# Causal attention in the last two chunks: probabilities of two cells added on GpSimd, one ones product for both

## The chip, the cores and the metric

One Trainium2 chip, one NeuronCore of it. The metric is the device time of one execution in microseconds (us). TensorE, VectorE, ScalarE, GpSimd and SP (which only issues DMAs here) run their own instruction queues, each in order, and wait for one another on semaphores.

## The reference, cut to what matters

```python
x = L0_attn_src                                      # (1, 2048, 128)
x = x + 0.5 * _L0_ffn_ref(_layernorm(x), ...)        # blockwise fp4, 352 wide
x = x + _L0_attn_ref(_layernorm(x), ...)             # linear attention, 16 heads of 64, and its MLP
x = x + 0.5 * _L0_ffn_ref(_layernorm(x), ...)        # fp4 again
x = x + 0.5 * _L1_ffn_ref(_layernorm(x), ...)        # relu layer, 512 wide
xe = _layernorm(x)
x = x + _L1_attn_ref(xe, ...)                        # causal, 16 heads; q = xe (8 a head), v of 32 a head
#   scores = q @ k.T + mask; attn = softmax(scores); o = attn @ v; xe + gelu(o) @ Wf + bf
x = x + 0.5 * _L1_ffn_ref(_layernorm(x), ...)
```

## The kernel before, in words

Rows of x are 16 tiles of 128. What every engine does is one list, `PLAN`, worked out on the host: `follow` walks it on each engine, and each engine issues its part of every step in that order. `first_pass` is fp4 and the sums of linear attention, `second_pass` (by `SECOND_ORDER`) the rest of linear attention with fp4 and relu layer of earlier tiles beside it, `causal` everything from there on.

Causal attention works on 4 chunks of 512 queries and 4 groups of 4 heads in a chunk: groups 0 to 15. A cell `(g, kb)` is group g against one block of 128 keys; chunk c has 4(c+1) blocks, so `CELLS` has 160 cells, and `GROUP_U[g]` is the first cell of a group (0, 4, 8, 12, 16, 24, 32, 40, 48, 60, 72, 84, 96, 112, 128, 144, 160). The last four cells of a group lie on the diagonal and have 512, 384, 256 and 128 queries. Each cell is two halves of two heads: `scores` (L1653, bf16 into a pair of PSUM banks, mask at L1660) and the exponential on ScalarE (L967, 1024 columns into `pr`, a ring of 3 cells). `values` (L1677: four heads side by side, each 32 columns of the array, fp32) is issued in the first half of the next iteration for the cell before, `sums` (L1692: the same with ones, for the softmax's denominators) in its second half. `values` adds in bank 6, `sums` in bank 7, over a group.

The softmax's maximum is found ahead: `max` (L1618, mask L1624) makes the scores the other way round, up to 512 keys by two heads, and VectorE reduces them (L1290). The `max` steps of a group are spread over the cells of the group before, ending `MAX_LEAD` = 4 cells before its first cell. `row_max` (L1300 to L1304, VectorE) joins them and splits the maximum in two bf16 parts, `turn_max` (L1636) turns them, ScalarE copies (L975), and four DMAs (L654) put them beside the queries.

Scores, maxima and most single steps (`IN_SETS`) take three pairs of PSUM banks in turn, in plan order (`set_of`); a step waits until the reader of the step three before is done.

Behind a group, `take_o` (L982) and `take_d` (L988) copy the banks out; denominators are gathered by DMA (L663), inverted (L1308), stored and spread (L670, L677), and GpSimd multiplies (`norm`, L803). `gelu` (L996), `wf` (L1706), and the relu layer (`f_stats`, `d_norm`, `d_turn` L1555, `d_hidden` L1565 and L936, `d_out` L1576, `d_add`) follow for each chunk. Keys and values of a chunk come from `e_stats`, `e_norm` (L1089), `e_turn`, `e_k`, `e_v`, `split`; `store_parts` and `load_queries` on SP (L627, L635, L645) store the bf16 parts and load keys and queries. SP's queue takes these, `load_maxima`, `gather_sums`, `store_inverse`, `spread_inverse` and the stores of x in plan order. Whatever fp4 and relu work of tiles 8 to 15 the second pass left is put by `last_tiles` into half-cell slots from -17 on (`TAIL_START`, `TILE_STEPS`); negative slots stand before the first cell.

## Time and profile before

| what | value |
|---|---|
| runs of the kernel | 1080.92, 1081.2, 1095.3 us; median 1081.2 |
| profiled execution | 1089.29 us, its span 1087.5 us |
| granted TensorE clock, mean | 0.948 |
| PE busy (matmuls) | 920.0 us, 85% |
| VectorE, ScalarE, GpSimd busy | 713.5, 513.0, 257.8 us |
| first exponential of a cell | 463.8 us |
| `take_o` of groups 7, 11, 14, 15 | 668.4, 850.3, 1013.8, 1053.7 us |

The device time includes some 2 us around the span. Times of rows are counted from the span's start. L12 is line 12 of the kernel; PE is TensorE's matmul, PEld its weight load, DVE VectorE, ACT ScalarE, POOL GpSimd, SPq the DMA issues of SP. Many instructions have operands in one big tensor, `arena`. "<-" at the end of a row names what ended the idle time before it.

### The profile page before, as it was taken

What the parts mean: (1) busy time and instruction counts of PE and PEld (TensorE: products, weight loads), DVE (VectorE), ACT (ScalarE), POOL (GpSimd) and SP (SyncE); (2) the same over time, 40 slices, a digit from 0 to 9 for tenths busy, and PEclk for the clock granted to TensorE, in tenths of its full rate; (3) what the DMA queues carried; (4) which work ended last, traced back from release to release, by engine and by line L of the source; (5) the groups of instructions that cost most, each with busy time, mean ns of one, the idle gap of its engine ahead of it and who ended that gap; (6) DMA issues with size and microseconds to landing.
All of it is one profiled execution on the core that took longest, in us unless ns stands there. A gap on an engine that the chain in (4) does not pass through costs nothing.

```text
span 1087.5 us, 19966 instructions
## 1 busy us (share of the span) xinstructions
PE 920.0 (85%) x7332; PEld 459.6 (42%) x7353; DVE 713.5 (66%) x1675; ACT 513.0 (47%) x884; POOL 257.8 (24%) x405
## 2 busy tenths in 40 slices
PE   2788888778888687798889899899899989999986
PEld 1444446565676466444323333233322223332225
DVE  7899953468876666775755588566488757676012
ACT  1133332234444232354565556656556656566772
POOL 1546420045554555421311001112000000000000
PEclk9999998999998887988999899999899999999997
DMA  5300000000000040041002300001500000000000
GB/s 183 67 14 1 1 0 1 1 1 1 1 2 1 1 79 10 2 81 20 23 11 58 54 8 24 2 12 35 74 2 11 12 1 15 7 10 5 12 2 10
DMA packets 30935, 23.20 MB, mean 21 GB/s; under 512 B 9609, under 2 KB 27897, under 8 KB 30840
## 3 DMA queue, kind: packets, MB, share of 16 engines
q1 hardware_dynamic: 29928, 21.39, 9.1%
q8 instruction: 61, 1.00, 0.4%
q10 hardware_dynamic: 912, 0.54, 0.2%
q14 instruction: 34, 0.28, 0.1%
HBM read 17.32 MB, written 4.34 MB: 20 GB/s over the span
## 4 chain that ended last, share of the span: by engine, by line
PE 61%; DVE 16%; ACT 7%; POOL 6%; issue 5%; DMA 3%; SPq 1%; ACTq 0%; DVEq 0%; POOLq 0%
PE psum L1677 11%; PE psum L1692 10%; PE psum L1653 7%; DVE arena L1290 5%; PE psum L1618 5%; PE psum L1565 3%; PE psum L1412 3%; PE psum L1371 2%; ACT arena L967 2%; PE psum L1576 2%; PE psum L1534 2%; PE psum L1422 2%; POOL rs L697 2%; DMA arena<-arena 2%; PE psum L1599 2%
## 5 line engine op out<-in xcount | busy, mean ns | idle before, releaser
L1290 DVE TENSOR_REDUCE arena<-psum 128x2 f32<-128x1024 f32 (+2 forms) x320 | 336.3, 1063 | 146.6 <-PE psum L1618 83.2
L967 ACT ACTIVATE arena<-psum 128x1024 f32<-128x1024 f32 (+3 forms) x320 | 286.7, 898 | 169.3 <-PE psum L1653 95.6
L697 POOL TENSOR_TENSOR rs<-ve,mhalf 128x1 f32<-128x1 f32 x128 | 70.7, 559 | 389.3 <-DVE ve L1084 388.8
L1677 PE MATMUL psum<-arena 128*32 128x512 f32 (+3 forms) x1280 | 153.2, 551 | 1.3 <-ACT arena L967 1.3
L1692 PE MATMUL psum<-arena,ones 128*32 128x512 f32 (+3 forms) x1280 | 153.7, 553 | 0.0
L1618 PE MATMUL psum<-arena 48*128 48x512 bf16 (+3 forms) x640 | 114.2, 358 | 25.9 <-ACT arena L967 13.8
L1653 PE MATMUL psum<-arena 50*128 50x512 bf16 (+3 forms) x640 | 116.8, 361 | 11.6 <-DMA arena<-arena 4.0
L1653 PEld LDWEIGHTS psum<-arena 50*128 50x128 bf16 x640 | 31.1, 93 | 200.8 <-issue 135.1
L936 ACT ACTIVATE rh<-psum,fb 128x128 f32<-128x128 f32 x128 | 36.5, 370 | 60.9 <-PE psum L1565 56.9
L803 POOL TENSOR_TENSOR arena<-arena 128x512 f32<-128x512 f32 x15 | 19.1, 1274 | 188.2 <-DMA arena<-scr_sums 188.2
L1371 PE MATMUL psum<-WguT,xqT 128*128 128x352 f32 x128 | 52.1, 536 | 7.0 <-DVE hb L1115 5.8
L1618 PEld LDWEIGHTS psum<-arena 48*128 48x128 bf16 x640 | 36.0, 94 | 46.2 <-ACT arena L967 19.3
L1565 PE MATMUL psum<-xdT,fW 128*128 128x128 f32 x256 | 43.1, 322 | 7.7 <-DVE arena L1290 3.7
L701 POOL TENSOR_TENSOR xv<-xv,xm 128x128 f32<-128x128 f32 x32 | 20.2, 631 | 123.0 <-DVE xv L1042 123.0
L1565 PEld LDWEIGHTS psum<-xdT,fW 128*128 128x128 f32 x256 | 38.2, 228 | 20.2 <-issue 15.8
L1677 PEld LDWEIGHTS psum<-arena 128*32 128x32 f32 x1280 | 25.4, 109 | 43.1 <-issue 38.3
L1338 PE MATMUL psum<-bias_rows,onesb 128*128 128x128 bf16 (+1 forms) x107 | 28.7, 268 | 12.5 <-ACT arena L996 4.3
L855 ACT ACTIVATE th<-psum 128x352 f32<-128x352 f32 x32 | 14.9, 464 | 49.9 <-PE psum L1371 49.8
L1576 PE MATMUL psum<-fW,rh 128*128 128x128 f32 x256 | 38.0, 295 | 0.0
L1462 PE MATMUL psum<-arena 128*128 128x256 f32 x128 | 37.4, 390 | 0.0
L1692 PEld LDWEIGHTS psum<-arena,ones 128*32 128x32 f32 x1280 | 25.5, 109 | 24.8 <-issue 20.1
L1392 PE MATMUL psum<-WdT,hqT 128*128 128x128 f32 (+1 forms) x192 | 32.6, 314 | 2.7 <-ACT hqT L849 2.7
(186 smaller groups left out, 1494.9 us busy)
## 6 DMA issues: line engine op xcount, KB each, us to landing
arena<-scr_parts SPq DMA_DIRECT2D x96, 64.0 KB
arena<-scr_sums SPq DMA_DIRECT2D x60, 64.0 KB, 2.0
scr_parts<-arena SPq DMA_DIRECT2D x12, 256.0 KB, 2.6
arena<-arena SPq DMA_DIRECT2D x124, 2.0 KB, 1.7
X<-in_L_attn_src_dram SPq DMA_DIRECT2D x4, 256.0 KB, 4.9
out_dram<-X SPq DMA_DIRECT2D x16, 64.0 KB, 1.6
arena<-in_c_zsel_dram SPq DMA_DIRECT2D x1, 512.0 KB, 3.8
arena<-in_L_attn_Wk_dram SPq DMA_DIRECT2D x1, 512.0 KB
```

Of the source, the lines that this page charges most:

```text
L697: v.tensor_tensor(rs[:, u, t:t + 1], ve[:, u, t:t + 1], mhalf[:, :], ALU.pow).then_inc(s_rstd[u], 1)
L936: v.activation(rh[:, n % 2, j, :], bank(bank_d(n, "d_hidden"))[:, P * j:P * j + P], ACT.Relu, bias=fb1[:, j:j + 1]).then_inc(s_relu, 1)
L967: v.activation(pr[:, u % RING, pp, :, 0:CH - off], both(("scores", n))[0][:, :, off:CH], ACT.Exp).then_inc(s_p, 1)
L1290: v.tensor_reduce(MXP[:, j, 2 * pp:2 * pp + 2, m], both(("max", g, pp, j, m))[0][:, :, 0:hi - lo], AX_X, ALU.max).then_inc(s_mxd, 1)
L1371: last = mm(bank(b + k)[:, 0:GI], xqT[:, n % 2, :], WguT[:, k, :], start=True, stop=True)
L1462: last = mm(o, Wq[:, P * j:P * j + P], XNT[:, GRP * g:GRP * g + GRP], start=False, stop=True, skip_group_check=True)
L1565: last = mm(bank(b)[:, P * j:P * j + P], fW1[:, P * j:P * j + P], xdT[:, n % 2, :], start=True, stop=True)
L1576: last = mm(bank(b)[:, P:2 * P], rh[:, n % 2, j, :], fW2[:, j, :], start=False, stop=(j == FJ - 1), skip_group_check=True)
L1618: last = mm(o[:, par, 0:w], QS[c % 2][r, hp, P * j:P * j + P], KK[m][r, hp, 0:w], start=True, stop=(m < c), skip_group_check=True)
L1653: last = mm(o[:, par, off:CH], KK[kb // TPC][r, hp, P * (kb % TPC):P * (kb % TPC) + P], QS[c % 2][r, hp, off:CH], start=True, stop=(kb < T ...
L1677: last = mm(bank(O_BANK)[VD * h:VD * h + VD, off:CH], V[kb // TPC][:, kb % TPC, GH * (g % GPC) + h, :], pr[:, u % RING, h // 2, h % 2, 0:C ...
L1692: last = mm(bank(D_BANK)[VD * h:VD * h + VD, off:CH], ones1[:, 0:VD], pr[:, u % RING, h // 2, h % 2, 0:CH - off], start=(kb == 0), stop=en ...
```

## The change

In chunks 2 and 3 (but for the last four cells of group 15) GpSimd adds the probabilities of a cell to those of the cell before (`add_probs`, two operations a pair of cells, planned at the second cell plus one), and `sums` runs once for the pair, in the second half of the iteration four behind its first cell. `pr` becomes a ring of 5, `GT` a ring of 6 groups, and `DN` shares its place with tables that are used up. `d_norm` and `e_norm` of the last part, and the two small operations that split `row_max`, go from VectorE to GpSimd. `gelu` is by group. `store_parts` and `load_queries` of a chunk go behind the maxima of the third group of the chunk before. The last part starts at slot -12: the maxima of group 1 no longer end before the first cell, tiles 12 to 15 start at slots 2, 6, 12, 18 at two slots a step, and inversions and norms come two cells later. In the second pass `e_stats` and `e_norm` of the first tiles move a little.

```diff
-                ("e_stats", 8, 1), ("den", 0), ("x_stats", 0, 1), ("x_turn", 1, 1), ("d_add", 6, 1),
-                ("e_norm", 8, 1), ("quotients1", 0, 1),
...
+                ("den", 0), ("x_stats", 0, 1), ("x_turn", 1, 1), ("d_add", 6, 1), ("e_stats", 6, 0),
...
-NORM_AT, GELU_AT = 4, 7
-RELU_START, RELU_TILE = 12, 4
+PAIRED_FROM = 2
+SUM_AT = 4
+INVERT_AT, NORM_AT, GELU_AT = 4, 6, 9
+RELU_START, RELU_TILE = 14, 4
+HELD = 6
...
-TAIL_START = {8: -16, 9: -16, 10: -15, 11: -14, 12: -17, 13: -11, 14: -7, 15: -2}
-MAX_START = {0: -16, 1: -8}
-SECOND_KEYS_START, SECOND_KEYS_EVERY = -12, 3
+FIRST_SLOT = -12
+TAIL = {8: (-11, 1), 9: (-11, 1), 10: (-10, 1), 11: (-9, 1), 12: (2, 2), 13: (6, 2), 14: (12, 2), 15: (18, 2)}
+MAX_LEADS = {1: 2, 2: 3, 3: 3, 4: 3}
+SECOND_KEYS_START, SECOND_KEYS_EVERY = -9, 3
...
-        RING = 3
+        RING = 5
...
+        SUMS = sorted([(a + (SUM_AT if pair else 1), a, pair)
+                       for g in range(MGROUPS) for a in range(GROUP_U[g], GROUP_U[g + 1])
+                       for pair in [g // GPC >= PAIRED_FROM and (g + 1 < MGROUPS or a < GROUP_U[g + 1] - TPC)]
+                       if not pair or (a - GROUP_U[g]) % 2 == 0])
...
+            max_end = [FIRST_SLOT + len(MAXES[0])] + [2 * GROUP_U[g] - 2 * MAX_LEADS.get(g, MAX_LEAD)
+                                                     for g in range(1, MGROUPS)]
+            for g in range(MGROUPS):
+                lo = max_end[g - 1] if g else FIRST_SLOT
                 for k, x in enumerate(MAXES[g]):
-                    slots.setdefault(MAX_START[g] + k, []).insert(0, ("max", *x))
...
+                    slots.setdefault(lo + (max_end[g] - lo) * k // len(MAXES[g]), []).append(("max", *x))
+                slots.setdefault(max_end[g], []).append(("row_max", g))
+                slots.setdefault(max_end[g], []).append(("turn_max", g))
+                if g % GPC == GPC - 2 and g + 2 < MGROUPS:
+                    slots[max_end[g]] += [("store_parts", g // GPC + 1), ("load_queries", g // GPC + 1)]
...
+            for a in PAIRED:
+                for pp in range(GP):
+                    put(a + 2, "add_probs", GP * PAIRED.index(a) + pp)
...
+                out += [x for x in here if x[0] in ("gelu", "add_probs")]
                 cut = (len(others) + 1) // 2
                 for i in range(GP):
+                    slot = slots.get(2 * u + i, [])
+                    out += [x for x in slot if x[0] == "row_max"]
                     if u < len(CELLS):
                         out.append(("scores", GP * u + i))
...
+                    out += [x for x in slot if x[0] == "max"]
+                    if i == 0 and 0 < u <= len(CELLS):
+                        out.append(("values", u - 1))
...
+                    for when, a, _ in SUMS:
+                        if (i, u) == (1, when):
+                            out.append(("sums", a))
...
+                    out += others[cut * i:cut * (i + 1)] + [x for x in slot if x[0] not in ("row_max", "max")]
...
+            def add_probs(n):
+
+                a, pp = PAIRED[n // GP], n % GP
+                w = [CH - P * max(kb - TPC * (g // GPC), 0) for g, kb in CELLS[a:a + 2]]
+                into = pr[:, a % RING, pp, :, w[0] - w[1]:w[0]]
+                pool.wait_ge(s_av, a + 1)
+                pool.wait_ge(s_p, GP * (a + 1) + pp + 1)
+                v.tensor_tensor(into, into, pr[:, (a + 1) % RING, pp, :, 0:w[1]], ALU.add).then_inc(s_ps, 1)
...
+            def row_max_parts(g):
+                pool.wait_ge(s_mxr, g + 1)
+                k = me.did(v.tensor_copy(MXH, MXS[:, :, :, 0]))
+                me.wait(k)
+                v.tensor_tensor(MXS[:, :, :, 1], MXS[:, :, :, 0], MXH, ALU.subtract).then_inc(s_mxn, 1)
...
-                if u >= RING:
-                    act.wait_ge(s_dn, u - RING + 1)
+                old = u - RING
+                if old in SUM_N:
+                    act.wait_ge(s_dn, SUM_N[old] + 1)
+                elif old >= 0:
+                    act.wait_ge(s_ps, GP * (PAIRED.index(old - 1) + 1))
+                    act.wait_ge(s_av, old + 1)
...
+                if u in PAIRED:
+                    pe.wait_ge(s_ps, GP * (PAIRED.index(u) + 1))
+                else:
+                    pe.wait_ge(s_p, GP * (u + 1))
```

## Rows read from the trace of the kernel before

**Rows 1.** Stretches: length; busy us of PE, PEld, DVE, ACT, POOL; clock; DMA share; GB/s
```profile
700.00:800.00 100.00, 93.36 (x844) 36.04 (x842) 59.93 (x82) 55.72 (x86) 13.72 (x23) 0.97 0.18 33
1000.00:1050.00 50.00, 48.74 (x450) 11.77 (x450) 3.33 (x7) 37.23 (x42) 1.28 (x1) 1.00 0.03 7
```

**Rows 2.** The same view, the stretch around the first cells
```profile
420.00:540.00 120.00, 98.48 (x971) 53.28 (x969) 85.81 (x195) 50.68 (x110) 37.56 (x58) 0.88 0.15 28
```

**Rows 3.** Groups of lines, 849-1012 us: busy, mean ns | idle before, releasers
```profile
L1290 DVE TENSOR_REDUCE arena<-psum 128x2 f32<-128x1024 f32 (+3 forms) x89 | 100.1, 1126 | 41.2 <-PE psum L1618 27.5 <-PE psum L1624 13.3
L967 ACT ACTIVATE arena<-psum 128x1024 f32<-128x1024 f32 (+3 forms) x95 | 90.0, 952 | 49.6 <-PE psum L1653 38.7 <-PE psum L1660 10.8
```

**Rows 4.** Instructions in time, one half-cell of group 12: start, duration, engine, line
```profile
885.65 0.39 PE L1653 MATMUL psum<-arena 50*128 50x512 bf16 x2
887.19 0.39 PE L1653 MATMUL psum<-arena 50*128 50x512 bf16 x2
887.42 0.38 PE L1618 MATMUL psum<-arena 48*128 48x512 bf16 x2
887.62 1.02 ACT L967 ACTIVATE arena<-psum 128x1024 f32<-128x1024 f32 x1 [0.52 <-PE psum L1653]
887.73 1.06 PE L1677 MATMUL psum<-arena 128*32 128x512 f32 x8
```

**Rows 5.** The same view, group 14: an exponential, and scores that waited for it
```profile
1010.22 0.60 ACT L967 ACTIVATE arena<-psum 128x512 f32<-128x512 f32 x1 [0.46 <-PE psum L1660]
1010.89 0.10 PEld L1653 LDWEIGHTS psum<-arena 50*128 50x128 bf16 x2 [0.62 <-ACT arena L967]
```

**Rows 6.** Chain that ended last, group 15: start, duration, what
```profile
1019.18 0.32 PE psum L1653 x2
1019.51 0.99 PE psum L1692 x8
1049.90 0.78 PE psum L1677 x8
1053.32 0.38 PE psum L1677 x8
```

**Rows 7.** Groups of lines of GpSimd, each shape apart
```profile
L701 POOL TENSOR_TENSOR xv<-xv,xm 128x128 f32<-128x128 f32 x32 | 20.2, 631 | 123.0 <-DVE xv L1042 123.0
L803 POOL TENSOR_TENSOR arena<-arena 128x512 f32<-128x512 f32 x15 | 19.1, 1274 | 188.2 <-DMA arena<-scr_sums 188.2
L783 POOL TENSOR_TENSOR X<-X,xe 128x128 f32<-128x128 f32 x16 | 7.2, 453 | 27.5 <-DVE xe L1089 27.4
L743 POOL TENSOR_TENSOR arena<-arena 127x1024 f32<-127x1024 f32 x1 | 2.4, 2355 | 0.0
L714 POOL CAST ident<-arena 128x64 bf16<-128x64 f32 x1 | 0.2, 237 | 0.0
```

**Rows 8.** Waits of TensorE's weight loads, 667 to 1053 us: total, times, longest
```profile
PEld psum L1636 <- DVE arena L1304: 3.4, 4, 0.8
```

**Rows 9.** Chain that ended last, 590 to 612 us, and a wait of that stretch
```profile
588.46 2.75 DMA scr_parts<-arena
591.22 0.29 SPq L635
595.40 0.64 SPq L654
597.35 7.90 DMA arena<-arena
...
PEld psum L1653 <- DMA arena<-arena: 4.5, 1, 4.5
```

**Rows 10.** VectorE in time around 771 us, and TensorE's wait
```profile
776.87 0.25 DVE L1308 RECIPROCAL arena<-arena 128x16 f32<-128x16 f32 x1 [5.23 <-DMA arena<-arena]
...
PE psum L1565 <- DVE arena L1290: 3.7, 1, 3.7
```

**Rows 11.** Chain that ended last, behind the last cell
```profile
1056.19 1.28 ACT L996
1057.48 0.64 ACT arena L996
```

142 lines of the change are left out of this document (74 added, 68 removed).

## Prediction

> **What bounds the kernel now.** I read the stretches first, then the groups of lines of the late part, then single instructions in order of time, then the waits. In the last two chunks TensorE is busy 93 to 97% of the time at nearly full granted clock, ScalarE 56 to 74%, VectorE 60% and in the last group 7% [rows 1]. The mean exponential and the mean row-maximum reduction each take about a microsecond, and both engines' idle time there is ended by TensorE [rows 3]. So from 667 us to 1053 us TensorE's queue is the bound. In the instructions, one half-cell runs scores, a maximum product, and `values` or `sums`, and the next half begins 1.54 us later [rows 4]. Scores plus maximum take 0.54 us of it (887.19 to 887.73), the four-head product 0.99 us, the pitch in the last group [rows 6]. Where no maxima are left a half-cell is 1.32 us [rows 6]. Ahead of that, from 420 to 540 us, nothing is full: TensorE 98.5 of 120 us at a clock of 0.88, VectorE 85.8 [rows 2]; that stretch is bound by handoffs.
>
> **Time base.** The profiled execution took 1089.3 us with a span of 1087.5; the median of the runs is 1081.2. All terms are differences in us, summed against 1089.3 and carried over to the median, 8.1 lower. A measurement of this kernel tells about 2%, 21.6 us, from no change.
>
> **1. One ones product for two cells.** Chunk 2 has 12 cells a group in four groups, chunk 3 has 16; all are paired but the last four cells of group 15: 24 + 24 + 6 = 54 pairs, so 54 of 160 sums go. A full one is worth 0.99; the last four cells of a group lose one of 384 and one of 128 columns, 0.78 + 0.38 [rows 6]. Groups 8 to 11: 4 x 0.99 + 1.16 = 5.1 each, 20.5. Groups 12 to 14: 6 x 0.99 + 1.16 = 7.1 each, 21.3. Group 15: 5.9. In all 47.7 of TensorE's queue.
>
> What is late once it is gone? The halves of a pair of cells are now scores-max-values, scores-max-sums, scores-max-values, scores-max. The fourth is 0.54 long. PSUM pairs rotate by three, so a maximum product takes the pair that the scores of the half before had. Those scores' exponential starts 0.43 behind them and takes 1.02 [rows 4], and the bank reaches TensorE 0.07 later (1010.82 to 1010.89) [rows 5]: 1.52 after the scores. In a full half the maximum comes at 1.54 + 0.23 = 1.77 and nothing waits; behind the short half it would come at 0.54 + 0.23 = 0.77, so it waits 0.75. TensorE takes its queue in order, so the whole queue waits. A pair gains 0.99 - 0.75 = 0.24. Full pairs with one maximum per half: 4 each in groups 8, 9, 10 and 6 each in 12, 13, 14, that is 30, so 7.2. The shorter cells on the diagonal have shorter exponentials; I take half of their 1.16 in six groups, 3.5. Group 11 has 32 maxima (the next group is of chunk 3) in 24 halves: 32 x 1.13 = 36 on VectorE [rows 3], as much as 24 halves of 1.54: nothing. In some short halves other steps (keys, relu layer) stand and fill the wait: 1. In group 15 `values` waits for the exponential of the half before, at 1.52 instead of 0.64: gain 0.11 in each of six pairs, 0.7. Term: **-12**. Bounds: 0, and -47.7 if no wait appears.
>
> **2. The additions on GpSimd.** Two of 128x1024 per pair. The nearest row is a two-input operation of 127x1024, 2.36; the 128x512 one is 1.27 [rows 7]. So 4.7 per pair, against 5.9 per pair of cells (6.16 - 0.24): GpSimd fits, with some 1.2 left. The sums come four cells behind the first cell of the pair, and a ring of five holds the tiles: the second addition ends 6.3 after the start of the pair's second cell, and three cells are 8.9. No wait there: **0**. The bound above is rival 4.
>
> What hangs on it is `row_max`. Its copy and subtraction go to GpSimd, and the plan puts the additions of cells U-6 and U-5 right ahead of them, U being the group's first cell. Counted from the start of cell U-5: `values` of cell U-6 ends at 1.6, so addition 0 runs 1.6 to 4.0 and addition 1 to 6.3, then two small operations (a cast of 64 columns is 0.24 [rows 7]) and handoffs, to 6.9. TensorE reaches `turn_max` after scores (2.08), maximum (1.54 + 1.52 = 3.06) and `values` (3.37 to 4.36), and stands until 6.9: 2.5 us, with scores, exponentials and all else of its queue behind it. Before, this wait cost 3.4 in four places in the whole late part [rows 8]. Other steps in that half (a layer's turn, a `wf`) cover some 0.4. Groups 9 to 15: 7 x 2.1 = **+15**. Bounds: 0 if GpSimd runs ahead of this, +25 if casts and handoffs take a microsecond more.
>
> Here the skill speaks against the change. The trace: on GpSimd a 128x128 two-input operation takes 0.63 beside VectorE's quantising chain and 0.45 in the other place [rows 7], 1.39 times. The Trainium skill (GPSIMD Engine Reference, Key points) says that GpSimd shares its SBUF interfaces with VectorE and is held up by VectorE instructions in a two-port mode or with two SBUF inputs. In the late part VectorE nearly only reduces out of PSUM [rows 3], which is neither, so I leave the additions at 2.36; with the factor it is rival 4.
>
> **3. Stores and loads of the keys, moved in SP's queue.** Before, they follow the last `split` of a chunk. Near 600 us the maxima of the next group are issued behind 12 loads and land after 7.90 us; TensorE waits 4.5 for them [rows 9], about 4.0 of it with nothing in flight (it ends at 605.25). Near 771 the gather of group 9's sums lands late, VectorE waits 5.23 for it, and TensorE 3.7 for VectorE [rows 10]. After, they are queued right behind a group's maxima, and the next gather is at least four cells off, over 15 us, against 2.8 for the stores and 24 issues of 0.3, 10 us, on the queue [rows 9]. Both waits go: **-8** (bounds 0 and -10). The spread of group 4's inverse now stands behind these loads, so `norm` waits on GpSimd; the turn that needs GpSimd next is four cells later, so 0 (at most +4).
>
> **4. First cells, tail and maxima rearranged.** Scores begin four slots after the first group's maximum row, and tiles 12 to 15 are spread over the cells behind at two slots a step. Work is the same; what can be gained is TensorE's 21.5 idle us of 420 to 540, and the half clock (0.12 x 120 = 14) [rows 2]. Against it: the rows of groups 0 to 4 have leads of two to four cells for a chain over VectorE, GpSimd, TensorE, ScalarE and four DMAs, of which the four issues of 0.64 alone take 2.5 [rows 9]. I take half the idle time: **-10**. Bounds: +8 (one such wait for each of four groups at 2) and -30.
>
> **5. Norms on GpSimd, gelu by group, invert and norm two cells later, e_norm order in the second pass.** The norms relieve VectorE of some 34 short operations, where it isn't the bound: 0 (-3 to +3, the relief or a turn that waits for GpSimd). Gelu has the same columns and the same table loads. At the end the table load (1.28) comes earlier but three gelus of 0.64 with it, so the first `wf` starts as before [rows 11]: 0.
>
> **Sum.** -12 + 15 - 8 - 10 = -15: 1089.3 to 1074, and 1081.2 to **1066**.
>
> **Rivals.**
> 1. The short half is free: part 1 pays in full, 36 more: 1030. For it: TensorE's all-idle time in this stretch is small now, and other steps may sit in the short halves more often. Against: the 1.52 of rows 4 and 5 can't shrink. Chance 0.12.
> 2. `turn_max` doesn't stand: GpSimd reaches the row early, or TensorE has as much other work. 15 less: 1051. For it: the leads leave room to be late. Against: the queue order. Chance 0.22.
> 3. The first part gives nothing (its tiles only fill cells that TensorE already fills), and the new stops lower the granted clock a little: +10 to +15, 1076 to 1083. For it: from 667 on a step moved in is a step added. Chance 0.20.
> 4. The slower side: the additions run beside VectorE at 1.39 x 2.36 = 3.28. From 2.95 on, two exceed 5.9 and GpSimd is the bound: 54 x (6.56 - 5.9) = 35, and `turn_max` 7 x 1.85 = 13 later; -15 + 48: 1114. Against: the fifteen 128x512 ones agree in mean with the 1024 one by size. Chance 0.08.
>
> The forecast (1058 to 1075) has 0.38. Left out of 1040 to 1088 are rivals 1 and 4, 0.20. Faster by over 2% (below 1059.6): rivals 1 and 2 and 0.04 of the forecast, 0.38. Slower: rival 4 and 0.02 of rival 3, 0.10. Within: 0.52.
>
> **What would show it.** Right: `sums` at about 106 cells' worth; a regular wait of some 0.75 of maximum products for the exponential, and cells of about 2.95 us; a wait of 2 us at the turn of groups 9 to 15 ended by GpSimd; additions of 2.36; no stop near 600 and 771; first exponential over 10 us sooner. Wrong: cells at 2.6 us (rival 1), no such wait at the turn (2), group 4 reached no sooner than before (3), additions over 2.95 (4).

## The result: slower by 5.2%, and the profile after

The changed kernel took 1142.6 us (median of 4 runs, 1134.6 to 1152.6), the kernel before 1081.1 beside it: a ratio of 1.052 (95% interval 1.040 to 1.063). The profiled execution took 1137.3 with a span of 1135.4. Forecast were 1066 and a range of 1040 to 1088; the sign was wrong too. Among runs of one kernel some are slower than the others by over 1.5%: the ratios leave these out, the medians don't.

Where the 47.9 us of span (1087.5 to 1135.4) went, by the starts of the first exponential of a group of cells (L967 before, L1022 after) and of the last `take_o`:

| stretch | before | after | difference | forecast |
|---|---|---|---|---|
| start to group 4 | 535.3 | 525.1 | -10.2 | -10 |
| groups 4 to 7 | 132.2 | 167.3 | +35.1 | -4 |
| groups 8 to 15 (the late part) | 386.2 | 407.6 | +21.4 | -1 |
| behind the last `take_o` | 33.7 | 35.4 | +1.7 | 0 |

The groups of lines, from the page of the kernel after (line, engine, operation, shapes, count, busy us, mean ns of one, idle time before and what ended it):

```profile
L832 POOL TENSOR_TENSOR arena<-arena 128x1024 f32<-128x1024 f32 (+2 forms) x108 | 222.1, 2074 | 114.1 <-PE psum L1735 88.1
L1752 PE MATMUL psum<-arena,ones 128*32 128x512 f32 (+3 forms) x848 | 105.0, 570 | 0.0
L1613 PE MATMUL psum<-ident,xd 128*128 128x128 f32 x32 | 10.8, 339 | 33.9 <-POOL xd L836 32.8
```

GpSimd now makes 108 additions; `sums` (L1752) has 848 products, 106 cells' worth. And TensorE stood 33 us ahead of a layer's turn, L1613, for a norm on GpSimd.

The late part as one stretch (us, busy time of each engine, then granted clock, DMA share, GB/s), of before and then of after, to be read against [rows 1]:

```profile
667.50:1053.70 386.20, 363.94 (x3374) 116.46 (x3374) 230.97 (x286) 242.18 (x311) 28.79 (x41) 0.98 0.07 15
```

```profile
692.40:1100.00 407.60, 331.92 (x2942) 111.08 (x2942) 224.79 (x260) 237.78 (x311) 262.15 (x175) 0.95 0.06 14
```

TensorE lost 432 instructions (54 pairs of eight) and 32.0 us of busy time. Its idle time (the stretch less busy) rose from 22.3 to 75.7, by 53.4. The difference is the +21.4. TensorE's waits there (engine, line, what it waited for: us in all, times, longest):

```profile
PE psum L1676 <- ACT arena L1022: 31.0, 41, 4.6
PE psum L1694 <- POOL arena L847: 20.6, 7, 5.8
PE psum L1735 <- ACT arena L1022: 7.5, 11, 0.9
```

The second is `turn_max` behind GpSimd. The first is the maximum product behind a short half, but not in all of the 41: two of them, 4.62 and 3.97 us, are TensorE waiting while ScalarE loads its table for the gelu of the chunk before, does it and loads the table back, and the kernel before has these two as well (3.98 and 3.97, in a row of 12.4 us in 16 times). The other 39 are 0.57 in the mean, and 0.72 where the short half ahead holds nothing but scores and a maximum product. The third is `values` waiting for its exponential; before the change that was 1.3 us. The row of before, one of the two gelu stops after, and two products behind short halves of group 12:

```profile
PE psum L1618 <- ACT arena L967: 12.4, 16, 4.0
...
730.54 1.28 ACT L1048 ACT_TABLE_LOAD   x1
731.83 2.19 ACT L1048 ACTIVATE arena<-arena 128x512 f32<-128x512 f32 x4
734.04 1.28 ACT L1022 ACT_TABLE_LOAD   x1
736.29 0.39 PE L1676 MATMUL psum<-arena 48*128 48x512 bf16 x2 [4.62 <-ACT arena L1022]
...
905.71 0.39 PE L1676 MATMUL psum<-arena 48*128 48x512 bf16 x2 [0.72 <-ACT arena L1022]
911.70 0.39 PE L1676 MATMUL psum<-arena 48*128 48x512 bf16 x2 [0.72 <-ACT arena L1022]
```

What one turn behind GpSimd looks like, in order of time (start, duration, what, [idle time before and its end]):

```profile
718.56 4.63 POOL L832 TENSOR_TENSOR arena<-arena 128x1024 f32<-128x1024 f32 x2
723.14 0.20 POOL L845 CAST arena<-arena 128x16 bf16<-128x16 f32 x1
723.42 0.22 POOL L847 TENSOR_TENSOR arena<-arena 128x16 f32<-128x16 f32 x1
...
723.70 1.02 PE L1694 MATMUL psum<-ident,arena 128*8 128x128 f32 x4 [5.80 <-POOL arena L847]
```

Two operations of 0.2 us stand behind 4.6 us of additions, and TensorE behind them. Stretches of six us before and after this stop show what it does to the clock (the last but two column):

```profile
711.90:717.90 6.00, 5.36 (x47) 1.56 (x39) 4.92 (x5) 3.95 (x5) 5.92 (x5) 1.00 0.01 3
723.70:729.70 6.00, 5.67 (x22) 1.54 (x23) 1.23 (x1) 1.60 (x2) 2.01 (x4) 0.50 0.01 1
```

Granted 1.00 before and 0.50 (1.2 GHz) after 5.8 us of standing still: 22 products in place of 47 in the same time.

Two stops ahead of the late part are larger than anything in the forecast. First the one near 472 us (TensorE and SP's queue in order of time):

```profile
465.24 1.47 SPq L650 DMA_DIRECT2D scr_parts<-arena  x3
468.96 4.12 SPq L658 DMA_DIRECT2D arena<-scr_parts  x12
473.12 4.14 SPq L668 DMA_DIRECT2D arena<-scr_parts  x12
...
487.78 0.72 PE L1676 MATMUL psum<-arena 48*128 48x512 bf16 x4 [15.47 <-DMA arena<-scr_parts]
```

Chunk 1's key loads are issued from 469 to 477 us, and the maxima of group 4 want them at 472.3. Second, the one from 603.4 to 626.6, of the same view:

```profile
599.35 4.12 SPq L658 DMA_DIRECT2D arena<-scr_parts  x12
603.51 4.97 SPq L668 DMA_DIRECT2D arena<-scr_parts  x12
608.53 0.66 SPq L693 DMA_DIRECT2D scr_sums<-arena  x1
621.09 1.71 SPq L700 DMA_DIRECT2D early<-scr_sums  x4
624.47 1.26 POOL L854 TENSOR_TENSOR arena<-arena,early 128x512 f32<-128x512 f32 x1 [24.74 <-DMA early<-scr_sums]
625.71 0.80 POOL L836 TENSOR_SCALAR xd<-X,mv,rs 128x128 f32<-128x128 f32 x1
...
626.57 0.47 PE L1613 MATMUL psum<-ident,xd 128*128 128x128 f32 x1 [23.20 <-POOL xd L836]
```

Read it upwards from the last row: TensorE's turn waits for a 0.80 us norm of the residual layer on GpSimd; that stands behind `norm` of group 4 (L854); that waits for the spread inverse; the spread was issued at 621.1, when the store of the inverse had landed; the store was issued at 608.5 behind 24 loads of keys. The DMA view of 596 to 624 us gives its landing (KB each, us from issue to landing), and above it the mean busy share of the DMA engines in 40 slices, in tenths:

```profile
DMA  9910004555555555555655555555555553000343
...
arena<-scr_parts SPq DMA_DIRECT2D x24, 64.0 KB
early<-scr_sums SPq DMA_DIRECT2D x4, 64.0 KB, 1.9
scr_sums<-arena SPq DMA_DIRECT2D x1, 8.0 KB, 12.5
```

The same 8 KB store lands in 1.4 us (median of the eight after it) with no loads before it.

### The profile page after: what moved, and what is told of

It is laid out like the page before. It is cut to its first block, busy times and chain, and to the rows that moved or that the text cites. A ratio compares the mean times of both kernels' runs of the same rounds, so it can differ in the third digit from the quotient of the medians.

```text
span 1135.4 us, 19349 instructions
## 1 busy us (share of the span) xinstructions
PE 880.4 (78%) x6900; PEld 449.0 (40%) x6921; DVE 694.8 (61%) x1609; ACT 507.7 (45%) x887; POOL 511.6 (45%) x579
## 4 chain that ended last, share of the span: by engine, by line
PE 50%; DVE 15%; POOL 12%; ACT 10%; issue 7%; DMA 3%; SPq 2%; ACTq 0%; POOLq 0%; DVEq 0%
PE psum L1735 9%; PE psum L1752 6%; DVE arena L1352 5%; PE psum L1711 5%; ACT arena L1022 4%; PE psum L1676 4%; POOL arena L832 4%; PE psum L1623 3%; PE psum L1470 3%; POOL rs L720 2%; PE psum L1429 2%; PE psum L1592 2%; PE psum L1480 2%; PE psum L1634 2%; PE psum L1657 2%
## 5 line engine op out<-in xcount | busy, mean ns | idle before, releaser
L1352 DVE TENSOR_REDUCE arena<-psum 128x2 f32<-128x1024 f32 (+2 forms) x320 | 335.3, 1063 | 219.0 <-PE psum L1676 118.1
L1022 ACT ACTIVATE arena<-psum 128x1024 f32<-128x1024 f32 (+3 forms) x320 | 282.1, 898 | 162.8 <-PE psum L1711 89.2
L832 POOL TENSOR_TENSOR arena<-arena 128x1024 f32<-128x1024 f32 (+2 forms) x108 | 222.1, 2074 | 114.1 <-PE psum L1735 88.1
L1752 PE MATMUL psum<-arena,ones 128*32 128x512 f32 (+3 forms) x848 | 105.0, 570 | 0.0
L1711 PEld LDWEIGHTS psum<-arena 50*128 50x128 bf16 x640 | 31.7, 93 | 176.9 <-issue 109.8
L1735 PEld LDWEIGHTS psum<-arena 128*32 128x32 f32 x1280 | 25.6, 109 | 46.9 <-issue 31.8
L724 POOL TENSOR_TENSOR hv<-hv,hm 128x352 f32<-128x352 f32 x32 | 29.8, 930 | 28.9 <-DVE hv L1098 28.9
L1613 PE MATMUL psum<-ident,xd 128*128 128x128 f32 x32 | 10.8, 339 | 33.9 <-POOL xd L836 32.8
```

The lines of the kernel that those rows point to most:

```text
L724: k = me.did(v.tensor_tensor(x, x, m, ALU.subtract))
L832: v.tensor_tensor(into, into, pr[:, (a + 1) % RING, pp, :, 0:w[1]], ALU.add).then_inc(s_ps, 1)
L1022: v.activation(pr[:, u % RING, pp, :, 0:CH - off], both(("scores", n))[0][:, :, off:CH], ACT.Exp).then_inc(s_p, 1)
L1352: v.tensor_reduce(MXP[:, j, 2 * pp:2 * pp + 2, m], both(("max", g, pp, j, m))[0][:, :, 0:hi - lo], AX_X, ALU.max).then_inc(s_mxd, 1)
L1711: last = mm(o[:, par, off:CH], KK[kb // TPC][r, hp, P * (kb % TPC):P * (kb % TPC) + P], QS[c % 2][r, hp, off:CH], start=True, stop=(kb < T ...
L1735: last = mm(bank(O_BANK)[VD * h:VD * h + VD, off:CH], V[kb // TPC][:, kb % TPC, GH * (g % GPC) + h, :], pr[:, u % RING, h // 2, h % 2, 0:C ...
```

## The experiments

Stages of the profiled executions, us. "Late" is from group 8's first exponential to the last `take_o`; idle is late less TensorE's busy time; stops are TensorE's longest near 470 and near 610; ratios are to the kernel before on the same chip, with the 95% interval. A dash is a stop that isn't there. The ratio of the changed kernel itself is known to 0.011, some 12 us. "By the ratios" below is the difference of two ratios, times 1083 us; where it is smaller than that, what an edit did is read from the stretches of the trace and not from the time.

| kernel | to group 8 | late | idle | end | stops | median | ratio |
|---|---|---|---|---|---|---|---|
| before | 667.5 | 386.2 | 22.3 | 33.7 | -, 4.0 | 1081.1 | 1 |
| after | 692.4 | 407.6 | 75.7 | 35.4 | 15.5, 23.2 | 1142.6 | 1.052 (1.040-1.063) |
| e1 | 678.9 | 409.5 | 72.8 | 33.0 | 14.6, 3.1 | 1123.3 | 1.040 (1.032-1.048) |
| e2 | 676.9 | 417.5 | 75.9 | 35.6 | 11.1, 6.5 | 1132.6 | 1.049 (1.043-1.055) |
| e4 | 692.0 | 396.6 | 65.0 | 35.7 | 13.8, 22.3 | 1127.4 | 1.043 (1.038-1.049) |
| e5 | 698.3 | 387.8 | 21.6 | 36.3 | 19.4, 24.8 | 1110.9 | 1.031 (1.023-1.038) |
| e6 | 677.3 | 412.6 | 75.7 | 35.6 | 6.2, 7.5 | 1122.8 | 1.033 (1.027-1.040) |
| e7 | 668.4 | 401.9 | 70.5 | 30.0 | 11.2, - | 1108.5 | 1.021 (1.017-1.026) |
| e8 | 680.5 | 382.2 | 19.2 | 31.7 | 14.5, 7.1 | 1090.7 | 1.005 (1.001-1.009) |
| e9 | 668.8 | 394.8 | 59.5 | 30.0 | 4.8, 4.5 | 1094.9 | 1.009 (1.006-1.012) |
| e10 | 676.1 | 377.9 | 55.5 | 33.4 | 12.9, 6.3 | 1089.2 | 1.003 (0.998-1.008) |
| e11 | 677.3 | 384.3 | 22.0 | 30.5 | -, 13.2 | 1097.1 | 1.014 (1.009-1.020) |
| e12 | 680.2 | 410.7 | 38.9 | 31.7 | 11.3, 5.6 | 1121.2 | 1.037 (1.032-1.043) |
| e13 | 677.2 | 413.0 | 75.7 | 35.6 | 14.2, 4.4 | 1126.8 | 1.043 (1.038-1.049) |
| e14 | 666.0 | 394.6 | 29.3 | 33.6 | -, 11.8 | 1095.7 | 1.010 (1.006-1.015) |
| e15 | 680.4 | 410.4 | 74.6 | 35.7 | 14.9, 4.9 | 1130.7 | 1.042 (1.036-1.049) |
| e16 | 691.3 | 379.5 | 55.6 | 36.6 | 15.0, 23.5 | 1117.8 | 1.029 (1.023-1.035) |
| e17 | 682.1 | 379.5 | 55.5 | 31.5 | 13.0, 7.3 | 1097.2 | 1.006 (1.001-1.011) |
| e18 | 670.0 | 378.6 | 56.5 | 31.8 | 3.9, 4.4 | 1083.7 | 0.997 (0.994-1.001) |
| e19 | 674.4 | 375.4 | 48.7 | 34.2 | 4.8, 6.3 | 1077.2 | 0.989 (0.985-0.992) |

One caution for the column "to group 8": e7, e8, e9, e10, e12 and e17 place keys, loads and norms of the first groups alike or nearly so, and their stop near 470 is 11.2, 14.5, 4.8, 12.9, 11.3 and 13.0. A single profile's front part can't be compared to better than some 10 us.

The table also shows what the turn waits cost beside their own length. In the six kernels that keep the row's split behind the additions on GpSimd (after, e1, e2, e6, e13, e15) the late part has 72.8 to 75.9 us idle and TensorE is busy 332 to 342 us of it, at a granted clock of 0.91 to 0.95. In the four that pair without these waits (e10, e16, e17, e18) it is 55.5 to 56.5 idle and 322 to 324 busy, at 0.98 to 0.99.

### First round: one part undone at a time

**e1, norms back on VectorE.**
```diff
-        POOL_NORMS = {x for x in PLAN[main:] if x[0] in ("d_norm", "e_norm")}
+        POOL_NORMS = set()
```


> The norms d_norm and e_norm of the last part go back to VectorE; all else as changed. Theory A (two stops in the first half of causal attention: 15.5 us at 472 us for key loads, 23.2 us at 603 us because d_norm stands on GpSimd behind norm, which waits for a DMA; they are the loss): the 23 us stop goes, the 15 us one stays, so about 22 us less than the changed kernel, some 1118 us. Theory B (the loss is the pairing itself in the last two chunks: additions, turn waits, short halves): within 5 us of the changed kernel.

19 us of the median came back, 13 by the ratios, less than the 22 expected. The 23.2 us stop shrank to 3.1, now for VectorE (the waits of 440 to 668 us):

```profile
PE psum L1676 <- DMA arena<-scr_parts: 14.6, 1, 14.6
PE psum L1613 <- DVE xd L1145: 3.1, 1, 3.1
```

The other stop, 14.6 us for the loads of chunk 1, has nothing to do with the norms.

**e2, stores and loads back behind the last `split` of a chunk.**
```diff
                         out.append((name, i - lag))
+                        if name == "split" and (i - lag) % TPC == TPC - 1:
+                            c = (i - lag) // TPC
+                            out += [("store_parts", c), ("load_queries", c)]
...
-                if g % GPC == GPC - 2 and g + 2 < MGROUPS:
-                    slots[max_end[g]] += [("store_parts", g // GPC + 1), ("load_queries", g // GPC + 1)]
...
```


> store_parts and load_queries go back behind the last split of their chunk, and the pace of the keys of chunks 2 and 3 is that of before; all else as changed. Theory A: chunk 1's loads are issued 3 cells sooner, the 15.5 us stop shrinks to under 3; group 4's inverse is stored and spread ahead of chunk 2's loads, so the 23.2 us stop goes too (in its place the old 4 us stop near group 6, for maxima behind loads): 30 to 35 us less, some 1106 us. Theory B: within 5 us.

A miss: 10 us by the medians, 3 by the ratios, in place of 30 to 35. Group 8 was reached 15.5 us sooner, and the late part was 9.9 longer. The 15.5 us stop turned into one of 11.1 a little earlier, where scores wait for the spread maxima (`arena<-arena` on SP) that were issued behind the same 24 loads; the 23.2 us stop into 6.5; and the one near 771 of [rows 10] came back larger, 9.0 near 797. In this place of the plan too, a small transfer that TensorE wants soon is behind the loads.

**e4, the split of the row maxima back on VectorE.**
```diff
                 v.tensor_reduce(MXS[:, :, :, 0], ..., AX_X, ALU.max, negate=True).then_inc(s_mxr, 1)
+                dve.wait_ge(s_mxr, g + 1)
+                me.wait(me.did(v.tensor_copy(MXH, MXS[:, :, :, 0])))
+                v.tensor_tensor(MXS[:, :, :, 1], MXS[:, :, :, 0], MXH, ALU.subtract).then_inc(s_mxn, 1)
...
```


> The two small operations that split the maximum row go back to VectorE; all else as changed. The wait at turn_max in groups 9 to 15 (20.6 us in 7 times) should fall to under 4 us: by both theories 15 to 18 us less than the changed kernel, some 1124 us. If the wait only moves (TensorE waits for something else later), the time is that of the changed kernel.

15 us less by the medians, 9 by the ratios. The late part fell by 11.0, and 8.4 us of turn waits stayed although GpSimd had nothing to do with the row any more. That left a question, answered by e7 and e10.

**e5, no pairs.**
```diff
-PAIRED_FROM = 2
+PAIRED_FROM = 4
```


> No cells are paired: one sums product per cell, no additions on GpSimd; all else as changed. Theory A with the forecast's terms for the late part (short halves leave -12 of 48, turn waits +15 and more): the pairing is worth nothing or costs up to 8 us, so 0 to 8 us less than the changed kernel, and the two early stops stay. Theory B: the loss is the pairing, 50 us less, some 1090 us. If the pairing pays as planned: up to 30 us more than the changed kernel.

Without what the change is about the kernel is 32 us faster by the medians and 23 by the ratios, and its late part is 387.8, as before the change. It missed what either theory gave, 0 to 8 and 50. So the pairing, in the form it has, costs some 20 us of the late part; the rest of the loss (1110.9 against 1080.5 beside it) lies in the front part.

### Second round: all side effects moved back

**e6, loads of keys placed elsewhere.** Chunk 1's behind group 1's maxima, chunk 2's behind the spread of group 4's inverse.
```diff
-                if g % GPC == GPC - 2 and g + 2 < MGROUPS:
-                    slots[max_end[g]] += [("store_parts", g // GPC + 1), ("load_queries", g // GPC + 1)]
+                if g in (1, 10):
+                    slots[max_end[g]] += [("store_parts", 1 + g // 5), ("load_queries", 1 + g // 5)]
+            slots.setdefault(2 * (GROUP_U[5] + INVERT_AT + 1) + 1, []).extend([("store_parts", 2), ("load_queries", 2)])
```


> Only two places change against the changed kernel: chunk 1's store and loads stand behind the maxima of group 1 (iteration 2 instead of 5), chunk 2's behind the spread of group 4's inverse (iteration 29 instead of 28). Queue theory: the 15 us stop falls to 5 or less, the 23 us stop falls to under 4 since the inverse is no longer behind the loads; 25 to 35 us less, 1108 to 1115 us. Rival (the DMA rings are simply loaded with the loads, whatever the order on SP's queue, and GpSimd's norm is late all the same): under 12 us less.

Both stops shrank (15.5 to 6.2, 23.2 to 7.5) and 20 us came back by the medians and the ratios, from the order of SP's queue alone. That is under the 25 to 35 expected: group 8 is reached 15.1 us sooner, and the late part is 5.0 longer. It is 2 to 10 us longer in every kernel of the table that has the early stops mended and the turn waits left (e1, e2, e6, e13, e15), with the same idle time and a lower clock. Why the clock is lower there no run shows.

**e7, e6 with the norms (e1) and the row's split (e4) on VectorE; the pairs stay.** **e8, the same without pairs** (`PAIRED_FROM = 4`).

> As the last one, and in addition the norms and the split of the maximum row go back to VectorE; pairs and additions stay. If the terms add up (stops 35, turn waits 11 to 15): 1095 to 1103 us. If one stop only gives way to the next: over 1110 us.

> As the last one without pairs: what is left of the change is the rearranged first part and small moves. Forecast term of part 4, -10 against the kernel before, and -4 for the stops that the kernel before had near 600 and 771: 1068 to 1076 us. Against e7 it shows what the pairing is worth when GpSimd does nothing else: my theory of late part (short halves hold TensorE 0.75 us, half the clock's gain lost) says e7 is 5 to 15 us slower than this; if pairing pays once the turn waits are gone, e7 is the faster.

e8 is within 1% of the kernel before: the rearranged first cells and tail by themselves gain nothing, where 9 to 17 us were expected. e7 is a miss as well, between its 1095 to 1103 and its 1110. It is 18 us slower than e8 by the medians, 17 by the ratios, and 19.7 in the late part of the profiles. So the pairing still lost time, though GpSimd had only additions to do. Its turn waits, 11.3 us in six times, were now put down to VectorE:

```profile
691.79 1.23 DVE L1353 TENSOR_REDUCE arena<-psum 128x2 f32<-128x1024 f32 x1 [0.64 <-PE psum L1686]
692.71 4.66 POOL L833 TENSOR_TENSOR arena<-arena 128x1024 f32<-128x1024 f32 x2
693.06 0.20 DVE L1363 TENSOR_REDUCE arena<-arena 128x16 f32<-128x48 f32 x1
693.29 1.81 DVE L1365 CAST arena<-arena 128x16 bf16<-128x16 f32 x1
695.14 2.26 DVE L1366 TENSOR_TENSOR arena<-arena 128x16 f32<-128x16 f32 x1
...
697.46 0.80 PE L1698 MATMUL psum<-ident,arena 128*8 128x128 f32 x3 [3.51 <-DVE arena L1366]
```

A cast and a subtraction of 16 columns take 1.81 and 2.26 us, and the subtraction ends with GpSimd's second addition (692.71 + 4.66 = 697.37, 695.14 + 2.26 = 697.40). The reductions in the same stretch, out of PSUM and of 48 columns of SBUF, take what they take without additions beside them (1.22 and 0.20).

**e9, e7 with the single steps of odd iterations in the second, short half.**
```diff
-                cut = (len(others) + 1) // 2
+                cut = 0 if u % 2 and u > GROUP_U[GPC * PAIRED_FROM] else (len(others) + 1) // 2
...
```


> As e7 (pairs stay), and in the odd iterations of the last two chunks every single step of the plan stands in the second half, which has no product of four heads. Theory: a short half waits 0.75 us for the exponential unless something else fills it, so some 20 of the 48 filled halves give 0.5 to 0.75 us each: 8 to 15 us less than e7. If the wait comes from something else (GpSimd, VectorE), the time is e7's within 3 us.

1094.9 (1092.6 to 1101.1), ratio 1.009 (1.006 to 1.012): 13.5 under e7, as expected. Of this the late part shows 7.1 (401.9 to 394.8): idle time fell by 11.0, and busy time rose by 3.9 (331.4 to 335.3) with the granted clock down from 0.96 to 0.94. So a step put where TensorE waits was nearly free.

### Third round: what the additions do to the rest

**e10, e7 with the additions cut to 8 of up to 512 columns a head.** It leaves out most of the sums of the second cells, so the denominators aren't the reference's; instructions, waits and handoffs are as in e7.
```diff
-                v.tensor_tensor(into, into, pr[:, (a + 1) % RING, pp, :, 0:w[1]], ALU.add).then_inc(s_ps, 1)
+                v.tensor_tensor(into[:, :, 0:8], into[:, :, 0:8], pr[:, (a + 1) % RING, pp, :, 0:8], ALU.add).then_inc(s_ps, 1)
```


> e7 with the additions cut to 8 columns of each head, so that they take some 0.3 us instead of 2.36; every wait stays. It leaves out most of the additions, so the denominators are too small. Theory C (the late part loses by TensorE's short half and by the granted clock that falls with it, GpSimd has nothing to do with it once the maximum row is split on VectorE): within 4 us of e7, 1104 to 1112 us. Rival D (the additions' length is what holds the ring of tiles, the sums or VectorE's memory port): most of the 18 us between e7 and e8 come back, 1091 to 1096 us.

19 us under e7 by the medians, 20 by the ratios: theory C fell, and rival D's amount came back. Turn waits 11.3 to 0.1, the late part 401.9 to 377.9, 24.0 less: 15.0 of idle time and 9.0 of busy time (331.4 to 322.4, the granted clock 0.96 to 0.98). The two small operations on VectorE, in e7 and then here:

```profile
L1366 DVE TENSOR_TENSOR arena<-arena 128x16 f32<-128x16 f32 x7 | 9.6, 1370 | 0.2
L1365 DVE CAST arena<-arena 128x16 bf16<-128x16 f32 x7 | 7.0, 995 | 0.2
```

```profile
L1365 DVE CAST arena<-arena 128x16 bf16<-128x16 f32 x7 | 1.3, 187 | 0.2
L1366 DVE TENSOR_TENSOR arena<-arena 128x16 f32<-128x16 f32 x7 | 1.2, 176 | 0.2
```

Eight and five times the duration, from the additions' width alone; e8, with no additions, has the same 187 and 176. Against e8 this is also the clean price of pairing without GpSimd's weight: busy 363.0 to 322.4 (-40.6), idle 19.2 to 55.5 (+36.3), net **-4.3**. The forecast's part 1 had -47.7, +36 and -12.

**e12, e7 with 47 products of 512 columns (four heads each, over a constant tile) put into the short halves.** They add to the denominators, which aren't the reference's.
```diff
+                        if (i, u) == (1, when + 1) and pair and LAST_SUM[CELLS[a][0]] != a:
+                            out.append(("filler", a))
...
```


> e7 with a ones product of 512 columns over a constant tile in every short half (47 of them, into the denominators' bank, so the denominators are wrong): TensorE gets back the 47 us of queue that the pairing had taken out, at the places where it now waits. Theory C: the filler takes the place of the 0.75 us wait and holds the clock up, so the time doesn't grow: e8's time within 5 us, 1086 to 1096 us, that is less than e7 although more is computed. Rival E (the clock plays no part, waits alone are the loss): the filler costs 0.99 for a wait of 0.75 to 0.9, so e7 plus some 5 us, 1110 to 1116 us.

1121.2 (1117.5 to 1124.4), 12.7 over e7 by the medians and 18 by the ratios, over what either theory gave (1096 and 1116). Had each cost its full 0.99, it would be 47. In the late part idle time fell from 70.5 to 38.9, busy time rose from 331.4 to 371.8, and the clock stayed at 0.96. So a short half has room for some 0.7 of an 0.99 product (31.6 of idle time in 47), and filling it didn't bring the clock back. The turn stops were still there (9.4 us), and where they are gone the clock is 0.98 (e10, e16).

**e13, the changed kernel with `norm` of group 4 five cells later.**
```diff
-                    put(end + NORM_AT, "norm", g)
+                    put(end + NORM_AT + (5 if g == 4 else 0), "norm", g)
```


> The changed kernel with one step moved: the norm of group 4 stands five cells later in the plan. Theory A: the 23 us stop is GpSimd waiting in this one norm for the spread inverse, which is behind chunk 2's loads; it goes, and the 15 us stop stays: about 20 us less than the changed kernel, 1114 to 1122 us. Rival: the loads themselves hold the kernel at that place (the next maxima, the next inverse), and the stop only moves: under 8 us.

1126.8 (1124.2 to 1130.5), ratio 1.043 (1.038 to 1.049): 16 us off the median, 9 by the ratios, with one instruction moved on GpSimd and nothing in the DMA queue; 20 were expected. The 23.2 us stop is gone, and two of 4.4 and 2.3 are left; group 8 starts at 677.2 in place of 692.4. The stop needs both: the late inverse that `norm` waits for, and the layer's `d_norm` queued behind `norm`.

**e11, the kernel before with chunk 2's loads at iteration 30, chunk 3's behind group 10's maxima, and the last gelu split by group.**
```diff
+                if g == 10:
+                    put(hi, "store_parts", 3)
+                    put(hi, "load_queries", 3)
+            put(30, "store_parts", 2)
+            put(30, "load_queries", 2)
...
```


> The kernel before with two small parts of the change alone: store and loads of chunk 2 at iteration 30 and of chunk 3 behind the maxima of group 10 (with the keys of chunk 3 paced to end there), and the last chunk's gelu of the three finished groups ahead of the last inversion. The stops at 601 us (4.0) and 774 us (3.7) should go, and the end behind the last cell should be some 3 us shorter as in e7: 7 to 11 us less than the kernel before. If the loads only collide with something else: no difference.

1097.1, ratio 1.014 (1.009 to 1.020), 1.4% slower where 7 to 11 us less were expected: a 13.2 us stop at 612.7, where VectorE's reciprocal waits for a gather behind the 24 loads.

```profile
624.65 0.25 DVE L1319 RECIPROCAL arena<-arena 128x16 f32<-128x16 f32 x1 [15.07 <-DMA arena<-arena]
```

The end behind the last `take_o` is 3.2 shorter (33.7 to 30.5), but not by the split gelu: TensorE's waits there are the same (the longest 4.3 and 3.1 before, 4.2 and 3.1 here), and its busy time fell from 20.1 to 17.0 with the granted clock at 0.89. The run e14, with the same gelu, ends in 33.6 at 0.75, as before. This run's end, and then e14's:

```profile
1061.60:1092.10 30.50, 17.03 (x113) 15.12 (x108) 10.33 (x32) 10.43 (x30) 2.25 (x4) 0.89 0.03 10
1060.60:1094.20 33.60, 20.13 (x116) 18.07 (x108) 10.33 (x32) 10.44 (x30) 2.25 (x4) 0.75 0.03 9
```

### Fourth round: mending it

**e15, the changed kernel with the inverses of groups 0 to 6 inverted, spread and applied two cells sooner.**
```diff
-                    put(end + INVERT_AT, "invert", g)
+                    sooner = 2 if g < GPC * PAIRED_FROM - 1 else 0
+                    put(end + INVERT_AT - sooner, "invert", g)
...
```


> The changed kernel with invert, store, spread and norm of groups 0 to 6 two cells sooner, as the kernel before had them (INVERT_AT 2, NORM_AT 4). Queue theory: group 4's small DMAs are through before chunk 2's 24 loads are issued; the 23 us stop goes, the 15 us one and the late part stay: 18 to 23 us less than the changed kernel, 1115 to 1122 us. Rival: the stop moves to another small DMA behind the loads (gather of group 5): under 10 us less.

1130.7, ratio 1.042 (1.036 to 1.049): the store now goes ahead of the loads, the 23.2 us stop is 4.9, and a turn stop of 4.4 came in. That is 10 us less by the ratios, where 18 to 23 were expected; group 8 is reached 12.0 us sooner.

**e16, the changed kernel with the row's split ahead of the additions in GpSimd's queue.**
```diff
-                out += [x for x in here if x[0] in ("gelu", "add_probs")]
+                out += [x for x in here if x[0] == "gelu"] + [x for x in slots.get(2 * u, []) if x[0] == "row_max"]
+                out += [x for x in here if x[0] == "add_probs"]
...
-                    out += [x for x in slot if x[0] == "row_max"]
+                    out += [x for x in slot if x[0] == "row_max" and i]
```


> The changed kernel with one order changed on GpSimd: in the seven iterations where both stand, the split of the maximum row comes ahead of the two additions. If the turn waits (20.6 us) are the queue behind the additions, they fall to under 4 us, and with them the stretches of half clock that follow each: late part (group 8's first exponential to the last take_o) 407.6 to some 380, 20 to 28 us less in all, 1112 to 1120 us. If VectorE is held by the additions as well, or the additions then come too late for the sums: less than half of that.

1117.8, 25 under the changed kernel by the medians and the ratios, by an order of seven pairs of small operations. Late 407.6 to 379.5: idle -20.1 (turn waits 20.6 to 1.6), busy -8.1 with the clock back at 0.98:

```profile
691.30:1070.80 379.50, 323.85 (x2946) 110.01 (x2942) 224.79 (x260) 237.81 (x312) 262.20 (x175) 0.98 0.06 15
```

GpSimd is as busy (262.2) as in the changed kernel; it only does what is waited for first. The late part is now 6.7 shorter than before the change.

**e14, the kernel before with chunk 2's and 3's loads behind the maxima of groups 6 and 10, and the gelu of e11.**
```diff
+                if g in (6, 10):
+                    put(hi, "store_parts", g // GPC + 1)
+                    put(hi, "load_queries", g // GPC + 1)
...
```


> The kernel before with the stores and loads of chunks 2 and 3 right behind the maxima of groups 6 and 10 (the change's places), inversions where they were, and the last chunk's gelu ahead of the last inversion. The 24 loads hold back every small DMA issued in the 15 to 20 us behind them; here the next one is the gather of group 5, four cells on, with two cells to spare. So the 4.0 and 3.7 us stops go and the end is 3 us shorter: 5 to 11 us less than the kernel before, 1074 to 1080 us. If the gather is caught after all: a stop of 3 to 8 us on VectorE near 612 us and no gain.

A miss: 1095.7, ratio 1.010 (1.006 to 1.015), with stops of 11.8 at 603 and 11.2 at 774. VectorE's reciprocal waits 13.7 us at 613.8 for a gather behind the loads, and TensorE for VectorE. The plans say why: the kernel before inverts two cells after a group's end, the changed one four, so the same place for the loads collides here and not there.

**e17, e15 + e16 + chunk 1's loads at group 1's maxima + norms on VectorE.**
```diff
-                if g % GPC == GPC - 2 and g + 2 < MGROUPS:
-                    slots[max_end[g]] += [...]
+                if g in (1, 6, 10):
+                    slots[max_end[g]] += [("store_parts", {1: 1, 6: 2, 10: 3}[g]), ("load_queries", {1: 1, 6: 2, 10: 3}[g])]
...
```


> All mends at once: inverses sooner, row ahead of the additions, chunk 1's loads behind the maxima of group 1, norms on VectorE; pairs, additions and the rearranged first part stay. By the terms: group 8 reached at 663 to 670 us, late part 380, end 31: 1076 to 1083 us, at or a little under the kernel before. If the pairing costs more than the turn waits and the clock: over 1090.

1097.2 over 11 runs (1081.3 to 1104.5), not faster than before, and a miss: 1076 to 1083 were expected. The late part kept its 379.5, and 13.0 us stood still near 470.

**e18, e17 with the four constants that place the head as before the change; e19, e18 with e9's filling.**
```diff
-FIRST_SLOT = -12
-TAIL = {8: (-11, 1), 9: (-11, 1), 10: (-10, 1), 11: (-9, 1), 12: (2, 2), 13: (6, 2), 14: (12, 2), 15: (18, 2)}
-MAX_LEADS = {1: 2, 2: 3, 3: 3, 4: 3}
-SECOND_KEYS_START, SECOND_KEYS_EVERY = -9, 3
+FIRST_SLOT = -16
+TAIL = {8: (-16, 1), 9: (-16, 1), 10: (-15, 1), 11: (-14, 1), 12: (-17, 1), 13: (-11, 1), 14: (-7, 1), 15: (-2, 1)}
+MAX_LEADS = {}
+SECOND_KEYS_START, SECOND_KEYS_EVERY = -12, 3
...
```


> This is the combined kernel (inverses sooner, row ahead of the additions, keys of chunk 1 loaded at the maxima of group 1, norms on VectorE) with one thing more put back: the four constants that place the first groups' maxima, the last tiles of the second pass and chunk 1's keys as the kernel before had them. Theory A (the stops of the combined kernel at 468 to 481 us come of scores that start before their keys are there, and nothing else of the front part costs): the 13 us stop goes and the first exponential of group 8 comes at about 667 to 672 instead of 682, the late part stays near 379.5, and the time is 1083 to 1088 less 10, some 1075 to 1080. Theory B (what the front part lacks is work for TensorE; each stop only changes its place): group 8 comes at 678 or later and the time stays at 1090 or above.

> The kernel of the run beside it with one thing more: in odd iterations of the last two chunks the single steps (layers' turns, wf, keys) are issued in the second half, which is the short one where a pair has no sums. In the kernel with everything moved back this was worth 13.5. If that gain came from filling the short halves, 5 to 10 less than the run beside it, as the late part has less idle time left with the row first (under 375). If it came mostly from the turn of the row maxima being relieved, it is 0 to 3 here.

e18: 1083.7 over 12 runs, 13.5 under e17 (9 by the ratios), and not told from the kernel before (0.994 to 1.001), with a first exponential of group 0 at 461.6 in place of 439.3 and one of group 8 at 670.0 in place of 682.1, which is in the 667 to 672 expected; the time is a little over its 1075 to 1080. So starting the cells 22 us later is no loss. That the loads then have other work beside them is an argument; no run separates it from the other constants. e19: 1077.2 over 12 runs (1064.1 to 1085.8; the profiled one is the slowest of them), ratio **0.989 (0.985 to 0.992)**: this version, which leaves no part of the computation out, beats the kernel before by 1.1%, which is little but clear of the noise. The 5 to 10 us expected against e18 came (6.5 by the medians, 9 by the ratios). Its waits in the late part:

```profile
PE psum L1678 <- ACT arena L1024: 23.4, 28, 4.6
PE psum L1713 <- DVE arena L1354: 7.5, 12, 2.4
PE psum L1737 <- ACT arena L1024: 7.5, 11, 0.9
...
PE psum L1696 <- POOL arena L849: 1.0, 2, 0.8
```

28 waits of the maximum products in place of 41 (the two for the gelu among them), and 1.0 at the turns in place of 20.6.

## Why the prediction was wrong

**Part 3 is the step that failed most.** It said that "the spread of group 4's inverse now stands behind these loads, so `norm` waits on GpSimd; the turn that needs GpSimd next is four cells later, so 0 (at most +4)". The order was seen rightly and priced wrongly, twice. The store issued behind the loads landed 12.5 us after its own issue, so the price was not their "24 issues of 0.3, 10 us, on the queue" alone (24 times 0.3 is 7.2; SP took 9.1). And the next thing that TensorE wants of GpSimd is not a `turn_max` four cells later but a `d_norm`, which part 5 of the same change had moved to GpSimd at a price of nothing. Neither alone makes the stop: e1 takes the norm away, e13 moves `norm` behind it, e15 moves the inverse ahead of the loads, and each leaves 3 to 7 us of the stop, takes 12 to 15 us off the way to group 8, and 9 to 13 off the time by the ratios. A wait on a queue has to be priced with everything that the change itself puts behind it. What part 3 gave as a gain did come (the stops of [rows 9] and [rows 10] are gone), 8 us against 23.

**Part 4 left a stop out.** -10 until group 4 came out as -10.2, but by luck: it is so with the 15.5 us stop for chunk 1's loads in it, which nothing in the forecast names: the scores start 23 us sooner (440.5 against 463.8) and the loads do not. And the gain was not kept: groups 4 to 7 took 35.1 more, of which the new stop less the old one is 19.2, and of the remaining 16 TensorE's busy time is 13.4 (118.6 to 131.9 us). It goes to the steps that were moved in there (1261 products in place of 1181) and to the lower clock (0.89 in place of 0.95); the two weren't told apart. That is the mechanism of rival 3, "the first part gives nothing", and e8 shows it nearly alone: the rearrangement with no pairs, the norms and the row's split on VectorE and other places for the loads, ratio 1.005. Putting the head's constants back gained 9 by the ratios (e18).

**Part 1: the mechanism was right, the sum a third of its size.** A maximum product behind a short half with nothing else in it waits 0.72, against 0.75, and two cells of group 12 take 5.99 us, against 5.92. All the waiting of pairing is 36.3 (e10 less e8) against the 36 that -12 means; about half of it is maximum products (13.3 to 30.6), the rest `scores`, most of it 5.7 for the relu layer on ScalarE and 5.3 for VectorE (0.7 in e8), and `values` (1.3 to 7.5). What was missing are 7 us of busy time: 54 removed sums are 47.7 at full clock, and 40.6 was what they gave. The forecast had no term for the clock. It is 0.99 in e8 and 0.98 in e10, which by an estimate from these two is some 3 of the 7; for the rest no run shows the cause.

**Part 2: additions 2.36, exactly as forecast** (128x1024: 2357 ns in 80), **and the turn waits 20.6 rather than 15.** The mechanism, casts behind two additions, is the one seen in the trace and the one that e16 takes away. Its price was not: behind the 5.8 us stop the granted clock is 0.50 for six us. e16 gives both at once, 20.1 of idle and 8.1 of busy time, 28 in place of 15.

**Part 5: the norms weren't free** (above; 0.80 us each on GpSimd). For the last gelu the 0 was right: e14 has it and the end of the kernel before, and where the end is shorter (e7, e11) the clock is higher. The changed kernel's end was 1.7 longer; there TensorE waits 4.2 us for a norm, 3.1 before.

**The rivals.** Rival 2 fell (turn waits of 20.6), rival 1 too (0.72 behind a short half). Rival 3 was right for the front part and for the clock, and short of both big stops; its +10 to +15 lead to 1076 to 1081, and not to 1083. Rival 4, at 1114, came nearest to the time, but by a mechanism that did not occur: the additions weren't slowed. The Trainium skill (GPSIMD Engine Reference, Key points) says that GpSimd shares its SBUF interfaces with VectorE and contends with VectorE's instructions in a two-port mode or with two SBUF inputs. It doesn't say there which of the two is held; I took it as a risk to GpSimd. The runs show the contention and who paid: the addition's mean is 2356 in e7 as in the changed kernel, and VectorE's subtraction (two SBUF inputs) went from 176 to 1370 ns and its cast from 187 to 995. With e7's 11.3 of turn waits that rule, read in the other direction, was worth a rival of its own.

The forecast's total then: -15 expected, +48 measured in the profiled executions (61 by the medians); of the 63 between, 39 lie in groups 4 to 7, 22 in the late part, 2 behind it.

What stays open: why the stop near 470 is 4.8 in one execution and 14.5 in another with the same plan up to there, how the 16 us of groups 4 to 7 divide between moved tiles and clock, and why the late part's clock is lower once the early stops are mended.

## What to carry to other kernels

When work is given to an idle engine, list what else is in that engine's queue and who waits for it; a 0.2 us operation that another engine needs belongs ahead of a 4.6 us pair that nobody needs soon (28 us here for one change of order). Bulk loads delay the small transfers issued behind them (11 to 15 us here behind 24 loads), so they go behind the last small transfer that is wanted soon, and each start that is moved sooner must be checked against the transfers it needs. And stops of some us of the bound engine can cost more than their length: with the turn waits gone, 20.1 us of idle time and 8.1 of busy time came back. A shorter stretch with the same work and the same waits can also be the clock alone, as the kernel's end was in e11.
